# PSUM banks of an attention kernel: from three and three to four and two, with paired row maxima

## The reference, cut to what matters

```
q = (src @ Wq + bq).reshape(B, T, N_HEAD, HEAD_DIM)
k = (src @ Wk + bk).reshape(B, T, N_HEAD, HEAD_DIM)
v = (src @ Wv + bv).reshape(B, T, N_HEAD, HEAD_DIM)
scores = jnp.einsum('bqhd,bkhd->bhqk', q, k) * scale
probs = jax.nn.softmax(scores, axis=-1)
attn = jnp.einsum('bhqk,bkhd->bqhd', probs, v).reshape(B, T, D_MODEL)
attn = attn @ Wo + bo
x = _layer_norm(src + attn, ln1_g, ln1_b)
...
ff_out = ff_out + jnp.where((expert_idx == e)[..., None], y, 0.0)
```

## Time and profile before

| | |
|---|---|
| median of 3 runs | 1274.57 us (1265.02 to 1293.35) |
| the profiled execution | 1264.88 us |
| its span | 1262.9 us |
| TensorE busy | 1069.3 us, 85% of the span |
| VectorE busy | 992.2 us, 79% |
| ScalarE busy | 790.1 us, 63% |
| GpSimd busy | 539.1 us, 43% |
| mean granted clock | 0.908 of full speed |

### The profile page before, as it was taken

The page is one execution under the profiler, slowest core; times in us unless marked ns, Lnnn a source line. Parts: engine busy times, 40 slices in busy tenths (PEclk is TensorE's granted clock), DMA queues, the critical chain, the costliest instruction groups (busy, mean ns, idle before and its releaser), DMA issues.

```text
span 1262.9 us, 20559 instructions
## 1 busy us (share of the span) xinstructions
PE 1069.3 (85%) x6007; PEld 399.3 (32%) x6007; DVE 992.2 (79%) x2429; ACT 790.1 (63%) x1670; POOL 539.1 (43%) x677
## 2 busy tenths in 40 slices
PE   4978879288998899988998988989989888979992
PEld 3755545022222222222222222222222222434440
DVE  7547785078999899999999998998999982376774
ACT  2413332103988888888878878888888788435551
POOL 6514333311223624634534435336246133475775
PEclk9557896555999999999999999999999999989996
DMA  5000000225224234234133243242342305275540
GB/s 155 9 0 1 0 0 0 62 39 101 61 45 101 70 69 103 64 75 98 49 82 91 51 95 91 48 102 70 69 102 66 73 2 170 72 228 164 166 131 15
DMA packets 101871, 94.33 MB, mean 75 GB/s; under 512 B 23102, under 2 KB 93183, under 8 KB 101769
## 3 DMA queue, kind: packets, MB, share of 16 engines
q1 hardware_dynamic: 94968, 80.19, 27.1%
q0 software_dynamic: 5504, 12.73, 2.8%
q10 hardware_dynamic: 1296, 0.20, 0.1%
HBM read 50.83 MB, written 42.92 MB: 74 GB/s over the span
## 4 chain that ended last, share of the span: by engine, by line
DVE 30%; PE 24%; POOL 15%; issue 8%; DMA 2%; SPq 2%; ACT 1%; POOLq 0%; ACTq 0%; DVEq 0%
DVE a_mx L1371 23%; PE ps_o L988 8%; PE ps_x L966 7%; POOL out L1515 5%; PE ps_s L973 3%; PE ps_m L931 2%; POOL a_qk L1214 2%; DMA ks<-stacks 2%; POOL a_parts L1223 1%; SPq L835 1%; PE ps_m L947 1%; POOL a_tnorm L1194 1%; POOL a_tnorm L1230 1%; POOL a_row L1227 1%; POOL a_tnorm L1219 1%
## 5 line engine op out<-in xcount | busy, mean ns | idle before, releaser
L1371 DVE TENSOR_REDUCE a_mx<-ps_x 128x1 f32<-128x512 f32 x1024 | 641.4, 683 | 83.4 <-PE ps_x L966 79.5
L1058 ACT ACTIVATE a_prob<-ps_s 128x512 f32<-128x512 f32 x1024 | 543.4, 604 | 86.2 <-PE ps_s L973 80.0
L966 PE MATMUL ps_x<-ks,a_qs 48*128 48x512 bf16 x1024 | 349.1, 403 | 73.5 <-DVE a_mx L1371 47.8
L973 PE MATMUL ps_s<-a_qs,ks 50*128 50x512 bf16 x1024 | 332.1, 390 | 21.1 <-ACT a_prob L1058 21.1
L988 PE MATMUL ps_o<-a_prob,vaug 128*32 128x512 f32 x2048 | 276.5, 612 | 0.0
L966 PEld LDWEIGHTS ps_x<-ks,a_qs 48*128 48x128 bf16 x1024 | 76.2, 95 | 394.3 <-DVE a_mx L1371 321.7
L1515 POOL DMA_INDIRECT out<-vaug,e_ids x76 | 84.7, 1114 | 21.7 <-issue 21.4
L973 PEld LDWEIGHTS ps_s<-a_qs,ks 50*128 50x128 bf16 x1024 | 74.3, 94 | 55.9 <-ACT a_prob L1058 52.8
L1146 POOL DMA_INDIRECT rows<-a_row,a_pos_i x64 | 64.3, 1005 | 56.8 <-DVE a_pos_i L1342 30.2
L1134 POOL CAST a_mx_parts<-a_mx 128x32 bf16<-128x32 f32 x32 | 6.6, 205 | 189.6 <-DVE a_mx L1371 189.6
L1156 POOL TENSOR_SCALAR a_vareps<-a_mv 128x4 f32<-128x4 f32 x16 | 3.2, 199 | 154.6 <-DVE a_mv L1281 154.6
(11 more groups left out here) (241 smaller groups left out, 1553.5 us busy)
## 6 DMA issues: line engine op xcount, KB each, us to landing
stacks<-a_parts SPq DMA_DIRECT2D x192, 128.0 KB, 2.4
a_qs<-stacks SPq DMA_DIRECT2D x64, 192.0 KB, 4.6
ks<-stacks SPq DMA_DIRECT2D x64, 192.0 KB, 5.0
x_tok<-rows SPq DMA_DIRECT2D x19, 520.0 KB, 4.0
rows<-vg_t SPq DMA_DIRECT2D x7, 520.0 KB, 4.1
a_qk<-in_L_ffn_W SPq DMA_DIRECT2D x13, 256.0 KB
a_z<-in_L_ffn_W SPq DMA_DIRECT2D x7, 256.0 KB
a_z_t<-in_L_ffn_W SPq DMA_DIRECT2D x6, 256.0 KB
```

The costliest lines, as they stand in the source:

```text
L966: pe.matmul(ps_x[:, bank(i + 1, n), :], qs[1 - r][own, pair, qt * P:(qt + 1) * P], ks[1 - r][own, pair, :], start=True, stop=True).then_in ...
L973: pe.matmul(ps_s[:, bank(i, n), :], ks[r][own, pair, kt * P:(kt + 1) * P], qs[r][own, pair, :], start=True, stop=True).then_inc(qk_mm, 1)
L1058: act.activation(prob[:, (s // 2) % RING, u % 4, :], ps_s[:, bank(i, u), :], ACT.Exp, scale=SCALE).then_inc(exp_done, EXP_STEP)
L1371: dve.tensor_reduce(mx[:, half, col:col + 1], ps_x[:, bank(i + 1, n), :], AX.X, ALU.max)\
```

## The change

The eight banks are dealt out anew: `ps_x` has four and `ps_s` two. The maxima of a slot's two units lie in two neighbouring banks, and VectorE reduces both in one instruction of 2 x 512 elements per partition that gives two results and raises `max_done` by 2. TensorE waits for `max_done` only at the even unit. The scores matmul of unit n waits for the exponential of unit n - 2 in place of n - 3. The experts take the fourth `ps_x` bank for what was the third `ps_s` bank.

```diff
-    BANKS = 3
+    MAX_BANKS, SCORE_BANKS = 4, 2
...
-        ps_s = ctx.enter_context(nc.psum_tensor("ps_s", [P, BANKS, S], F32))
-        ps_x = ctx.enter_context(nc.psum_tensor("ps_x", [P, BANKS, S], F32))
+        ps_s = ctx.enter_context(nc.psum_tensor("ps_s", [P, SCORE_BANKS, S], F32))
+        ps_x = ctx.enter_context(nc.psum_tensor("ps_x", [P, MAX_BANKS, S], F32))
...
-        banks = ([ps_s[:, 0, :], ps_s[:, 1, :], ps_s[:, 2, :], ps_x[:, 0, :]], ps_x[:, 1, :], ps_x[:, 2, :], ps_o[:])
+        banks = ([ps_s[:, 0, :], ps_s[:, 1, :], ps_x[:, 3, :], ps_x[:, 0, :]], ps_x[:, 1, :], ps_x[:, 2, :], ps_o[:])
...
-        def bank(b, n):
-
-            return (UNITS * b + n) % BANKS
+        def pair_bank(n):
+
+
+            return n % MAX_BANKS // 2 * 2
...
-            def bank_free(done, b, n, step=1):
-
-                wait(pe, done, (b * UNITS + n + 1 - BANKS) * step)
-
             def maxima_of(i, r, n):
 
                 pair, qt, hh = maxima_unit(n)
                 own = slice(HALF_ROWS * hh, HALF_ROWS * hh + HROWS)
-                bank_free(max_done, i + 1, n)
-                pe.matmul(ps_x[:, bank(i + 1, n), :], qs[1 - r][own, pair, qt * P:(qt + 1) * P],
+                if n % 2 == 0:
+                    wait(pe, max_done, (i + 1) * UNITS + n + 2 - MAX_BANKS)
+                pe.matmul(ps_x[:, pair_bank(n) + hh, :], qs[1 - r][own, pair, qt * P:(qt + 1) * P],
                           ks[1 - r][own, pair, :], start=True, stop=True).then_inc(mx_mm, 1)
 
             def scores_of(i, r, n, pair, kt):
 
                 own = slice(HALF_ROWS * (n % 2), HALF_ROWS * (n % 2) + KROWS)
-                bank_free(exp_done, i, n, EXP_STEP)
-                pe.matmul(ps_s[:, bank(i, n), :], ks[r][own, pair, kt * P:(kt + 1) * P],
+                wait(pe, exp_done, (i * UNITS + n + 1 - SCORE_BANKS) * EXP_STEP)
+                pe.matmul(ps_s[:, n % SCORE_BANKS, :], ks[r][own, pair, kt * P:(kt + 1) * P],
                           qs[r][own, pair, :], start=True, stop=True).then_inc(qk_mm, 1)
...
-                            act.activation(prob[:, (s // 2) % RING, u % 4, :], ps_s[:, bank(i, u), :],
+                            act.activation(prob[:, (s // 2) % RING, u % 4, :], ps_s[:, u % SCORE_BANKS, :],
...
-                            dve.wait_ge(mx_mm, UNITS * (i + 1) + n + 1)
-                            dve.tensor_reduce(mx[:, half, col:col + 1], ps_x[:, bank(i + 1, n), :], AX.X, ALU.max)\
-                               .then_inc(max_done, 1)
+                        dve.wait_ge(mx_mm, UNITS * (i + 1) + n + 2)
+                        dve.tensor_reduce(mx[:, half].rearrange("p (h m) -> p h m", h=2)[:, :, col:col + 1],
+                                          ps_x[:, pair_bank(n):pair_bank(n) + 2, :], AX.X, ALU.max).then_inc(max_done, 2)
```

More of the change, by code:

```diff
@@ L1361, in body @@
                     if on(i, 1):
[L1362 to L1369, removed]
-                            dve.wait_ge(mx_mm, UNITS * (i + 1) + n + 1)
-                            dve.tensor_reduce(mx[:, half, col:col + 1], ps_x[:, bank(i + 1, n), :], AX.X, ALU.max)\
-                               .then_inc(max_done, 1)
+                        n = 2 * s
+                        pair, qt, _ = maxima_unit(n)
+                        half, col = pair // (PAIRS // 2), pair % (PAIRS // 2) * T + qt
+                        if n == 0:
+                            wait(dve, msplit_step, 4 * i + 2)
+                        if n == UNITS // 2:
+                            wait(dve, msplit_step, 4 * i + 4)
+                        dve.wait_ge(mx_mm, UNITS * (i + 1) + n + 2)
+                        dve.tensor_reduce(mx[:, half].rearrange("p (h m) -> p h m", h=2)[:, :, col:col + 1],
+                                          ps_x[:, pair_bank(n):pair_bank(n) + 2, :], AX.X, ALU.max).then_inc(max_done, 2)
             steps(nc.vector, body, B)
```

## The result

The changed kernel takes 1333.5 us (median of 4 runs, 1328.1 to 1340.1), the one before 1277.5 us (median of 4, 1265.0 to 1293.4): a ratio of 1.048 with a 95% interval of 1.038 to 1.057, slower. The profiled execution took 1340.1 us with a span of 1338.3, that is 75.4 us more than the span before.

The account below looks back on a forecast made before the run. VectorE was taken to mostly set the pace before, the two-bank score loop after; 15 passes at +3.0 us (+45), pass 15 +7 and pass -1 -2 sum to +50 on 1264.9, 1315 us, range 1278 to 1345.

Parts of the forecast that it names:

- The loop: Scores, exponential, release, values, next scores: with two score banks a round takes 2.97 us in middle passes, 2.94 in pass 15.
- The small jobs: Copies, transposes and other short work between the rounds of a middle pass: 4.0 us a pass on top of the rounds.
- the jobs of 0.6 us behind odd slots: Remaining jobs of 0.6 us or less lie where TensorE waits for the exponential, 0.8 us or more: they add nothing.
- The joined reduction: On VectorE, one reduction of 1024 elements takes 1213 ns; a pair gains 0.07 us, 2.2 us per pass.
- Rival 1: VectorE keeps the pace and the shorter reductions show: 1230 us, or 1201 by the page's 120 cycles; chance 0.07.
- Pass -1: The pass ahead of pass 0, VectorE's alone, gets 2 us shorter.
- Pass 15 and the clock: The scores-only last pass gets 7 us longer, and TensorE, waiting a little more, keeps 2.4 GHz.
- The total: Whole kernel: +50 us on the profiled execution's 1264.9, giving 1315 us, read as 4.0% slower.
- rival 3: The pairs of maxima banks bind as well: 2 us more per pass, about 1340 us; chance 0.10.
- Rivals 2: No change within 2%: new waits fall into time TensorE already spends waiting for VectorE; 1280 us, chance 0.16.

Follow-up runs that it names:

- the kernel cut by columns: The changed kernel with each values matmul split, columns 0 to 255 behind the even slot and 256 to 511 behind the odd one; 1326.5 us.

## Why the prediction was right, point by point

**The loop** was right in every term: 2.97 us in a middle round and 2.94 in pass 15 at full clock. That it and nothing else makes the loss of the passes is shown by the kernel with two score banks alone.

**The small jobs** on top of it, 4.0 us a pass, were right in the sum but for 0.3 us: 52.1 us measured against 51.8, +49.8 us over 15 passes against +45. By the starts of the values in TensorE's timeline (500 to 553 us) "v" added 1.36 us (1.33 forecast), "mx1" 0.17 (0.17) and "at" 0.67 (0.71), but the four rounds with "wo", "q" and "k" (537.46 to 551.16) 1.8 in place of 1.3. The stretch with "v" and the two with "q" and "k" were named with their costs, and that the jobs of 0.6 us behind odd slots cost nothing is seen in the round of 2.97 us that holds the transpose of 512.91 (values at 511.38 and 514.35), and from the other side in the kernel cut by columns, where they cost their length.

**The joined reduction** was priced right: 1226 ns against 1213, and two in 2.35 us (516.47 in VectorE's timeline of the changed kernel) are 1.13 us each after the overlap. The price of an element came from a reduction of 2048 that doesn't read PSUM; that it carries over was assumed, and held within 13 ns. That it would not show was right: undoing it changed nothing. Rival 1 priced its worth at 35 us, on the condition that VectorE still sets the pace; that condition wasn't met. Its support, 322 us of waits on the reduction against 53, was weaker than it looked, since much of the 322 was the values' own time.

**Pass -1** gained 2.3 us, 2 forecast.

**Pass 15 and the clock** is the step that failed. I wrote that the scores-only pass had TensorE busy 83% of the time at clock 1.00, "so a TensorE that waits a little more should keep 2.4 GHz". It did not: in the pass's first 7 us TensorE was busy 76% and the clock 0.90, and then 0.50 for most of the pass. A busy share alone does not tell when: with two score banks alone TensorE was busy 77 to 79% in the first 27 us, and the clock stayed. The +7 us forecast were +21.3, of which the kernel with idle matmuls shows 11.4 to be the clock; the other 9.9 are the loop, 3 more than its term. The price per round stood in my reach: at half clock the values, which are a term of the loop, take 1.87 in place of 1.00, and the kernel before has such a row (values at 310.61, the next matmul at 312.47, 1.86 us). I took the last row at which nothing had happened for a bound on where something would.

**The total**: +50 forecast, +69.8 measured from the first reduction on or 75.4 with the stretch ahead of it. Of the 25 us beyond the forecast 14 are pass 15, 5 the middle passes, 5.6 the stretch ahead and 1 the rest. By medians it is +56.0, 4.4%, and by the ratio 4.8%, where 4.0% was forecast. The time alone would not have told: 1333.5 lies just above the 1300 to 1330 that the forecast had for itself, and nearer rival 3's 1340 (whose sum is off, too: 2 us in 15 passes are 30, not 26). Rivals 2 and 3 fell: two score banks alone are as slow, and single reductions in four banks are no faster.

## What to carry to other kernels

Before taking a buffer from a ring, write down the closed loop through it: from the release of a buffer, through everything that stands in the producer's in-order stream up to the next fill, to the consumer's release of it. One buffer less added one consumer's step here, 0.49 us a round, however idle that consumer's engine looks (ScalarE was 82% busy), and a gain on another engine does not count until this loop is shorter than that engine's. And work that costs nothing may be lying in the very wait that one means to remove: cost it again with the cover gone. In a phase with one ring idle, lend its buffers to the other.

## What the runs showed of the hardware

- TensorE's clock fell from 2.4 to 1.2 GHz in a pass in which TensorE waited more, and less work for it can cost time: pass 15 was 11.4 us shorter with 64 idle matmuls in it (6.8 against the other two kernels with two score banks); bf16 values, a third as long on TensorE (0.33 us where the clock was 1.00), took 0.6 us off the changed kernel's middle pass and left the one before at 49.0 for 48.8, at a mean clock of 0.74 and 0.77.
- Four fp32 matmuls with 32 output rows each and 512 columns take 1.00 us side by side and two of them 0.99; at 256 columns four take 0.57 (550.54 less 549.97 in the timeline of the kernel cut by columns).
- A reduction of 2 x 512 elements out of two PSUM banks with two results takes 1.226 us alone and 1.13 back to back, two single ones 1.20: the saving is 0.07 us.
- With six banks to read from, ScalarE starts an exponential every 0.477 us, 1.91 a round.
- A wait that the profile puts on a weight load includes the time for which TensorE streams the matmuls ahead of it: 0.84 us behind the values at 505.32 in the changed kernel and at 501.28 in the one before, put down to "issue" in one and to VectorE in the other.
